# Selective-scan kernel: another table of places for the marks, the output additions, the convolution and the softplus

## The chip, the cores and the metric

One core of a Trainium2 chip runs the whole program. The metric is the time of one execution on the device in microseconds; smaller is better. The time of a run is that of this one core.

## The reference, cut to what matters

The input is x of 4 x 1024 tokens by 256. It is normalised over its last axis, and two branches start from it: eight Mamba layers, and a mixture of eight experts with one expert per token. The result is x + s * silu(g), with s from the Mamba branch and g from the experts. Only the Mamba branch is touched here. One layer is:

```python
xz = einsum('bld,ed->ble', x, Wi); xin, z = split(xz, 2)
xin = silu(causal_conv(xin, cw, cb))               # 4 taps, 512 channels
x_dbl = einsum('blc,ec->ble', xin, Wx)             # rank 16, B 16, C 16
delta = softplus(einsum('blr,cr->blc', dt_raw, Wdt) + bdt)
h = h * exp(d_t[..., None] * A) + (d_t * u_t)[..., None] * B_t[:, None, :]
y = einsum('bcn,bn->bc', h, C_t)                   # 16 states
y = (y + u * Dp) * silu(z)
x = x + einsum('blc,dc->bld', y, Wo)
```

## The kernel before, in words

The program has three blocks: `experts`, `mamba` and `finish`. `mamba` takes most of the time, and it alone changes.

**Units and steps.** `mamba` works in 64 units: 8 layers, 4 sequences, 2 halves of 512 tokens. Units with an even number start a sequence (h = 0), odd ones continue it (h = 1) and begin each scan from a carry. A unit has 64 steps, written (n, j): state n from 0 to 15, block j of 128 channels from 0 to 3. Step (n, j) is number k = 4n + j. While unit U is scanned, the same steps also prepare unit U+1 (the "late" work) and unit U+2 (the "early" work), and finish unit U-1. Every engine has one queue of instructions in order, and the order is written out by hand: at each step an engine does its regular work and then whatever the tables at the top of the file (L75 to L85) place there. A place with n of 16 or more belongs to the following unit, so (17, 0) is step (1, 0) of the next one.

**The regular work of a step.**
- GpSimd (POOL, L768) multiplies du by a broadcast row of B into one of 8 drive buffers, so it is at most 8 steps ahead of the scan.
- ScalarE (ACT, L800, `exponent`) writes the decay exp(delta * A) into one of two PSUM buffers `ps_d`. At step k it makes the decay of step k + 2 and waits for scan k.
- VectorE (DVE, L962, `scan`) does the scan of 512 tokens into `state`, which has two buffers of four blocks. The first scan of state n therefore waits until TensorE has turned all four tiles of state n - 2.
- TensorE (PE) turns a tile of the state of n - 1 into the ring `ps_r` (L1118, `turn_state`), and turns the weighted product back into `ps_y` (L1125, `turn_back`).
- ScalarE (L807, `weigh`) reads the ring, multiplies by C and writes `prod`.

**The ring.** `ps_r` has two PSUM buffers, used in turn by all that TensorE hands to ScalarE or VectorE. An item waits until the item two before it has been read. Between the turned states stand the other items, placed by `RING_AT` (L75): `X0` to `X3` and `Z0` to `Z3` (input projection), `C3` (the convolution of channel block 3, on TensorE), `XD` (L1185) and `BC` (the projection to rank, B and C), `DT0` to `DT3` (delta), `O0` and `O1` (output projection, L1206), `CNT` (a count of marks). ScalarE reads an item one step after its place; `CNT`, `O0` and `O1` are read by VectorE where `ALIVE_AT` and `ADD_AT` say.

**The other work on VectorE.** `mark_over` (L971, L973, `MARK_AT`) marks values over a limit; `CNT` sums the marks; `keep_alive` (L984, `ALIVE_AT`) turns the count into a mask; `add_x` (L1066, `ADD_AT`) adds an output block to the residual; `gate` (L1060, `GATE_AT`) makes the four gated blocks, for which `skip_y` on TensorE (`SKIPY_AT`) waits; `conv` (L997 for the first tap, L1001 for the other three, `CONV_AT`) does 12 instructions for channel blocks 0 to 2; `softplus` (L1020, L1023, L1027, L1030, `SOFT_AT`) has two times four parts; `make_du` (L1010, `DU_AT`) has two parts, and POOL's first drive of the next unit waits for the first part, its third drive for the second.

**The other work on ScalarE.** At `SILU_AT` it does silu of the convolution (`silu_u`, L835), silu of z (`silu_z`, L839) and loads the other table again (L913). `silu_u` waits for the last convolution instruction. In the queue, `exponent` of a step stands ahead of the silus and `weigh` behind them:

```python
exponent(U, h, k)                       # k = CB * n + t + 2
if (n, t) == SILU_AT:
    silu_u(U, kind, U + 1); silu_z(U, h, kind)
    nc.scalar.preload_act_table_set(TABLE)
late(...); early(...)
weigh(U, h, kind, ("S", n - 1, t), U, n - 1, t)
```

**The other work on POOL.** `halo` (L747, L749, `HALO_AT`) waits for the last convolution instruction and for `C3`; `mask_x` (L739, `XM_AT`) waits for `keep_alive`; `keep_carry` (L754) copies the last column of a state. All stand in one queue with the drives.

**SP's queue** issues the DMAs. In the first unit of a layer its load of w_out (L630) waits until `O1` is in the ring, and the rows of B for states 8 to 15 (`load_brep`, L654) stand behind it.

## Time and profile before

| what | value |
| --- | --- |
| median of 3 runs | 7821.57 us (7820.64 to 7832.61) |
| the profiled execution, its own time | 7820.31 us |
| its span, first to last instruction | 7818.5 us |
| granted TensorE clock, mean of the span | 0.991 |
| busy: PE, PEld, DVE, ACT, POOL | 6939.0, 4775.6, 6646.4, 6434.1, 5911.4 us |

The page of the profile gives each engine's busy time and share of the span. Four engines are busy between 76% and 89%, so no share alone names the bound. The views that do are the busy time by stretch (one unit at a time), the waits, and the order of instructions by time on each engine inside one unit. A row of the order by time has the start, the time from the first start to the last end, the engine, the line, what is written and read, and in brackets the idle time before it with what ended it.

### The profile page before, as it was taken

What the parts mean: (1) busy time and instruction counts of PE and PEld (TensorE: products, weight loads), DVE (VectorE), ACT (ScalarE), POOL (GpSimd) and SP (SyncE); (2) the same over time, 40 slices, a digit from 0 to 9 for tenths busy, and PEclk for the clock granted to TensorE, in tenths of its full rate; (3) what the DMA queues carried; (4) which work ended last, traced back from release to release, by engine and by line L of the source; (5) the groups of instructions that cost most, each with busy time, mean ns of one, the idle gap of its engine ahead of it and who ended that gap; (6) DMA issues with size and microseconds to landing.
All of it is one profiled execution on the core that took longest, in us unless ns stands there. A gap on an engine that the chain in (4) does not pass through costs nothing. (4 is left out here: it accounts for less than half of the span.)

```text
span 7818.5 us, 143762 instructions
## 1 busy us (share of the span) xinstructions
PE 6939.0 (89%) x40051; PEld 4775.6 (61%) x40051; DVE 6646.4 (85%) x6454; ACT 6434.1 (82%) x10306; POOL 5911.4 (76%) x4899
## 2 busy tenths in 40 slices
PE   4978999999989998999998998989999999999987
PEld 3646666666666666666666666666666666666665
DVE  2249888988988998889889888988898898889888
ACT  1238888888888888888888888888888888888886
POOL 2128878887878888788877887887888788887875
PEclk9989999999999999999999999999999999999998
DMA  5111111111111111111111111111111111111112
GB/s 172 34 39 39 39 38 47 44 39 39 42 44 42 39 39 42 47 40 40 39 47 42 38 40 41 46 42 38 40 47 42 39 38 42 44 43 38 41 37 89
DMA packets 226304, 355.78 MB, mean 46 GB/s; under 512 B 43680, under 2 KB 82368, under 8 KB 225376
## 3 DMA queue, kind: packets, MB, share of 16 engines
q1 hardware_dynamic: 222096, 336.91, 15.9%
q0 software_dynamic: 3408, 9.33, 0.3%
q8 instruction: 365, 5.98, 0.3%
q14 instruction: 435, 3.56, 0.2%
HBM read 325.00 MB, written 21.14 MB: 44 GB/s over the span
## 5 line engine op out<-in xcount | busy, mean ns | idle before, releaser
L768 POOL TENSOR_TENSOR drive<-du,brep 128x512 f32<-128x512 f32 x4096 | 5499.6, 1372 | 725.9 <-DVE du L1010 359.7
L800 ACT ACTIVATE ps_d<-delta,cur 128x512 f32<-128x512 f32 x4096 | 2845.3, 695 | 453.7 <-DVE state L962 434.8
L807 ACT ACTIVATE prod<-ps_r,bcT 128x512 f32<-128x512 f32 x4096 | 2807.7, 686 | 242.3 <-PE ps_r L1118 237.3
L1118 PE MATMUL ps_r<-ident,state 128*128 128x128 f32 x16384 | 2551.6, 279 | 321.8 <-ACT prod L807 176.1
L962 DVE TENSOR_TENSOR_SCAN state<-ps_d,carry,drive 128x512 f32<-128x512 f32 x2048 | 2503.0, 1264 | 310.6 <-PE ps_r L1118 275.9
L962 DVE TENSOR_TENSOR_SCAN state<-ps_d,drive 128x512 f32<-128x512 f32 x2048 | 2389.7, 1206 | 301.0 <-PE ps_r L1118 237.7
L1125 PE MATMUL ps_y<-ident,prod 128*128 128x128 f32 x16384 | 2467.5, 275 | 25.9 <-ACT prod L807 25.9
L1125 PEld LDWEIGHTS ps_y<-ident,prod 128*128 128x128 f32 x16384 | 1929.0, 142 | 664.7 <-issue 514.0
L1118 PEld LDWEIGHTS ps_r<-ident,state 128*128 128x128 f32 x16384 | 1834.4, 141 | 768.0 <-ACT prod L807 495.1
L1166 PE MATMUL ps_r<-xm,w_inz_sb 128*128 128x512 f32 x1024 | 508.9, 620 | 91.8 <-ACT prod L807 91.8
L1158 PE MATMUL ps_r<-xm,w_inx_sb 128*128 128x512 f32 x1024 | 508.3, 620 | 25.9 <-ACT prod L807 14.3
L1206 PE MATMUL ps_r<-relu,w_out_sb 128*128 128x512 f32 x1024 | 472.5, 604 | 59.9 <-ACT prod L807 57.2
L1001 DVE SCALAR_TENSOR_TENSOR xc<-xpad,taps,xc 128x512 f32<-128x512 f32 x576 | 513.9, 892 | 2.7
L754 POOL COPY carry<-state 128x4 f32<-128x4 f32 x512 | 222.5, 435 | 218.1 <-DVE state L962 215.9
L1199 PE MATMUL ps_r<-xdbl,w_dt_sb 16*128 16x512 f32 x512 | 291.0, 649 | 86.0 <-DVE xres L1066 41.7
L1206 PEld LDWEIGHTS ps_r<-relu,w_out_sb 128*128 128x128 f32 x1024 | 184.1, 189 | 273.4 <-issue 216.6
L1166 PEld LDWEIGHTS ps_r<-xm,w_inz_sb 128*128 128x128 f32 x1024 | 174.4, 190 | 272.3 <-ACT prod L807 136.9
L1158 PEld LDWEIGHTS ps_r<-xm,w_inx_sb 128*128 128x128 f32 x1024 | 175.3, 190 | 196.2 <-issue 153.8
L427 ACT ACTIVATE hid<-ps_t,b_sb 128x128 f32<-128x128 f32 x312 | 84.8, 382 | 225.5 <-PE ps_t L388 225.5
L1185 PE MATMUL ps_r<-u,w_x_sb 128*48 128x512 f32 x512 | 235.2, 603 | 34.2 <-ACT u L835 34.2
L355 POOL DMA_INDIRECT ys_dram<-yb,row x39 | 37.4, 959 | 292.6 <-DVE yb L447 292.6
L1136 PE MATMUL ps_y<-u,skip 128*128 128x512 f32 x512 | 241.6, 594 | 9.4 <-DVE relu L1060 9.3
(136 smaller groups left out, 4574.7 us busy)
## 6 DMA issues: line engine op xcount, KB each, us to landing
brep<-bc_dram SPq DMA_DIRECT2D x1024, 256.0 KB, 3.3
w_sb<-w SPq DMA_DIRECT2D x8, 1024.0 KB, 17.5
w_all<-w SPq DMA_DIRECT2D x8, 1024.0 KB, 12.7
xs_dram<-nothing SPq DMA_DIRECT2D x1, 5011.5 KB, 35.9
xb<-xs_dram SPq DMA_DIRECT2D x39, 128.5 KB, 2.0
w_all<-x SPq DMA_DIRECT2D x1, 4096.0 KB, 14.7
w_inx_sb<-w_in SPq DMA_DIRECT2D x8, 512.0 KB, 4.0
w_inz_sb<-w_in SPq DMA_DIRECT2D x8, 512.0 KB, 4.4
```

Source lines behind the costliest of these rows:

```text
L768: nc.gpsimd.tensor_tensor(drive[:, k % DRIVE, :], du[:, j, :], brep[:, n % BREP, :], ALU.mult).then_inc(drive_set, 1)
L800: nc.scalar.activation(ps_d[:, k % 2, :], delta[h][:, j, :], ACT.Exp, scale=cur[h][:, a:a + 1]).then_inc(decay_set, 1)
L807: nc.scalar.activation(prod[:, t, :], ps_r[:, item_place(U, h, kind, item), :], ACT.Copy, scale=bcT[(h + 1) % 2 if item[1] == "prev" else ...
L962: nc.vector.tensor_tensor_scan(state[n % 2][:, j, :], ps_d[:, k % 2, :], drive[:, k % DRIVE, :], carry[:, n, j:j + 1] if h == 1 else 0.0, ...
L1001: step = nc.vector.scalar_tensor_tensor(xc[:, j, :], xpad[:, j, tap:tap + T], w, xc[:, j, :], ALU.mult, ALU.add)
L1118: last = nc.tensor.transpose(out[:, j * P:(j + 1) * P], state[n % 2][:, j, t * P:(t + 1) * P], ident[:])
L1125: last = nc.tensor.matmul(ps_y[:, j, t * P:(t + 1) * P], prod[:, t, j * P:(j + 1) * P], ident[:], start=False, stop=True, is_transpose=Tru ...
L1136: last = nc.tensor.matmul(ps_y[:, j, :], skip[:, j, :], u[:, j, :], start=True, stop=True, skip_group_check=True)
L1158: last = nc.tensor.matmul(out, w_inx_sb[:, k, j * P:(j + 1) * P], xm[h][:, k, :], start=(k == 0), stop=(k == DB - 1))
L1166: last = nc.tensor.matmul(out, w_inz_sb[:, k, j * P:(j + 1) * P], xm[hf][:, k, :], start=(k == 0), stop=(k == DB - 1))
L1199: nc.tensor.matmul(out, w_dt_sb[:, j * P:(j + 1) * P], xdbl[0:RANK, :], start=True, stop=True).then_inc(ring_ready, 1)
L1206: last = nc.tensor.matmul(out, w_out_sb[:, j, k * P:(k + 1) * P], gated[:, j, :], start=(j == 0), stop=(j == CB - 1))
```

## The change

Only the tables of places change. No instruction is added or taken away and no shape changes; `LOW_AT` is a new name that nothing in the kernel reads. `SILU_AT` goes one step later. The marks, the alive mask and both additions come to lie at (3, 3) to (4, 3); the gates are all at (1, 1). The convolution of a unit begins at (6, 2) instead of (5, 2), and four of its 12 instructions instead of three lie in the next unit. `C3` goes from (1, 0) to (2, 3). The softplus begins at (9, 2) instead of (7, 3), and the second part of `make_du` goes from (14, 3) to (15, 2).

```diff
-RING_AT = {"CNT": (3, 0), "O0": (4, 1), "O1": (5, 3), "XD": (4, 2), "BC": (7, 3), "DT0": (6, 0), "DT1": (6, 2), "DT2": (8, 0),
-           "DT3": (9, 2), "Z0": (10, 1), "Z1": (11, 3), "Z2": (14, 1), "Z3": (15, 0), "X0": (5, 0), "X1": (8, 3),
-           "X2": (10, 3), "X3": (14, 2), "C3": (17, 0)}
-SILU_AT, EXP_AT, LN_AT = (4, 2), [(7, 0), (10, 1)], [(8, 3), (11, 3)]
-MARK_AT, ALIVE_AT, ADD_AT = [(2, 1), (2, 2)], (3, 1), [(4, 3), (6, 1)]
+RING_AT = {"CNT": (4, 0), "O0": (3, 3), "O1": (4, 2), "XD": (4, 3), "BC": (11, 3), "DT0": (7, 2), "DT1": (7, 3),
+           "DT2": (10, 2), "DT3": (10, 3), "Z0": (9, 1), "Z1": (9, 3), "Z2": (13, 3), "Z3": (15, 0), "X0": (5, 3),
+           "X1": (7, 0), "X2": (8, 3), "X3": (13, 0), "C3": (18, 3)}
+SILU_AT, EXP_AT, LN_AT = (4, 3), [(9, 0), (12, 1)], [(9, 1), (13, 0)]
+MARK_AT, ALIVE_AT, ADD_AT = [(3, 3), (4, 0)], (4, 2), [(4, 1), (4, 3)]
 PE_CONV, DVE_CONV = [3], [0, 1, 2]
-GATE_AT, SKIPY_AT = [(1, 1), (1, 2), (1, 2), (1, 2)], [(1, 1), (1, 3), (1, 3), (1, 3)]
-SOFT_AT = [(7, 3), (8, 3), (9, 3), (10, 2), (10, 3), (11, 3), (14, 2), (14, 3)]
-CONV_AT = [(5, 2), (5, 2), (6, 0), (6, 2), (9, 2), (10, 1), (12, 2), (12, 3), (15, 1), (17, 0), (17, 3), (19, 0)]
-DU_AT = [(14, 3), (14, 3)]
-HALO_AT, XM_AT = (3, 2), (5, 1)
+GATE_AT, SKIPY_AT = [(1, 1), (1, 1), (1, 1), (1, 1)], [(1, 2), (1, 2), (1, 3), (1, 3)]
+LOW_AT = [(4, 1), (8, 2)]
+SOFT_AT = [(9, 2), (9, 3), (10, 3), (12, 3), (13, 1), (13, 3), (14, 2), (14, 3)]
+CONV_AT = [(6, 2), (7, 2), (7, 3), (8, 0), (9, 0), (9, 2), (10, 2), (11, 1), (18, 2), (18, 2), (19, 2), (19, 3)]
+DU_AT = [(14, 3), (15, 2)]
+HALO_AT, XM_AT = (4, 2), (5, 2)
```

## Rows read from the trace of the kernel before

**Rows 1.** The page's busy time of each engine.

```profile
PE 6939.0 (89%) x40051; PEld 4775.6 (61%) x40051; DVE 6646.4 (85%) x6454; ACT 6434.1 (82%) x10306; POOL 5911.4 (76%) x4899
```

**Rows 2.** Units 26, 27: us; PE, PEld, DVE, ACT, POOL busy; clock, DMA, GB/s.

```profile
3477.70:3589.40 111.70, 101.78 (x600) 70.03 (x601) 99.53 (x97) 98.69 (x157) 90.53 (x82) 1.00 0.16 40
3589.40:3702.80 113.40, 101.97 (x601) 69.83 (x600) 102.12 (x95) 98.50 (x156) 91.16 (x68) 1.00 0.15 39
```

**Rows 3.** Waits over the whole span: total us, times, longest us.

```profile
DVE state L962 <- PE ps_r L1118: 513.6, 262, 11.1
...
DVE xres L1066 <- PE ps_r L1206: 138.8, 67, 3.9
```

**Rows 4.** Order by time on ScalarE in unit 26: at C3, around the silus.

```profile
3488.70 0.69 ACT L827 ACTIVATE xc<-ps_r,taps 128x512 f32<-128x512 f32 x1 [2.24 <-PE ps_r L1177]
...
3507.15 0.70 ACT L800 ACTIVATE ps_d<-delta,cur 128x512 f32<-128x512 f32 x1
3507.86 1.28 ACT L835 ACT_TABLE_LOAD   x1
...
3514.18 0.69 ACT L807 ACTIVATE prod<-ps_r,bcT 128x512 f32<-128x512 f32 x1
3514.77 0.69 ACT L800 ACTIVATE ps_d<-delta,cur 128x512 f32<-128x512 f32 x1
```

**Rows 5.** Order by time on VectorE: unit 23 at the silus, unit 26 to (7, 0).

```profile
3169.82 0.69 DVE L1066 TENSOR_TENSOR xres<-xres,ps_r 128x512 f32 x1 [1.80 <-PE ps_r L1206]
3175.66 3.63 DVE L962 TENSOR_TENSOR_SCAN state<-ps_d,carry,drive 128x512 f32<-128x512 f32 x3 [5.16 <-PE ps_r L1118]
...
3501.17 6.77 DVE L962 TENSOR_TENSOR_SCAN state<-ps_d,drive 128x512 f32<-128x512 f32 x6
3510.28 0.69 DVE L1066 TENSOR_TENSOR xres<-xres,ps_r 128x512 f32 x1 [2.34 <-PE ps_r L1206]
3515.98 3.45 DVE L962 TENSOR_TENSOR_SCAN state<-ps_d,drive 128x512 f32<-128x512 f32 x3 [5.01 <-PE ps_r L1118]
...
3531.84 3.45 DVE L962 TENSOR_TENSOR_SCAN state<-ps_d,drive 128x512 f32<-128x512 f32 x3 [1.90 <-PE ps_r L1118]
```

**Rows 6.** Order by time on TensorE in unit 26: C3, CNT, O0, XD, DT0.

```profile
3484.90 3.60 PE L1177 MATMUL ps_r<-xpad,conv_w 128*128 128x512 f32 x8
...
3498.86 1.04 PE L1149 MATMUL ps_r<-over_mark,minus_ones 128*128 128x512 bf16 x4
...
3506.38 3.67 PE L1206 MATMUL ps_r<-relu,w_out_sb 128*128 128x512 f32 x8 [0.77 <-ACT prod L807]
...
3511.22 3.61 PE L1185 MATMUL ps_r<-u,w_x_sb 128*48 128x512 f32 x8 [0.30 <-ACT u L835]
...
3526.42 1.12 PE L1199 MATMUL ps_r<-xdbl,w_dt_sb 16*128 16x512 f32 x2 [0.18 <-DVE xres L1066]
```

**Rows 7.** Durations in ns, min/median/max, of four of VectorE's lines.

```profile
L997 DVE TENSOR_SCALAR xc<-xpad,taps x192: 514/646/1928, 482.2 to 7550.3; 128x512 f32<-128x512 f32 x192
...
L1001 DVE SCALAR_TENSOR_TENSOR xc<-xpad,taps,xc x576: 716/752/5805, 482.7 to 7574.0; 128x512 f32<-128x512 f32 x192
...
L971 DVE TENSOR_SCALAR over_mark<-xres x64: 658/661/687, 470.2 to 7455.2; 128x1024 bf16 x60, 128x1024 bf16<-128x1024 f32 x4
...
L1020 DVE TENSOR_SCALAR low<-soft x128: 659/666/1661, 505.8 to 7633.5; 128x1024 f32<-128x1024 f32 x128
```

**Rows 8.** Order by time on VectorE: step (1, 0) of units 26 and 15.

```profile
3483.43 1.09 DVE L1001 SCALAR_TENSOR_TENSOR xc<-xpad,taps,xc 128x512 f32<-128x512 f32 x1
...
2235.38 5.80 DVE L1001 SCALAR_TENSOR_TENSOR xc<-xpad,taps,xc 128x512 f32<-128x512 f32 x1
```

**Rows 9.** Order by time on POOL: halo and mask in unit 26; drives in unit 24.

```profile
3499.06 0.11 POOL L749 MEMSET xpad<- 128x12 f32 x1 [6.86 <-DVE xc L1001]
...
3507.98 2.35 POOL L739 TENSOR_TENSOR xm<-xres,alive 128x1024 f32<-128x1024 f32 x1
...
3304.93 2.51 POOL L768 TENSOR_TENSOR drive<-du,brep 128x512 f32<-128x512 f32 x2 [6.10 <-DMA brep<-bc_dram]
```

## The prediction

> **What bounds the kernel now.** The page comes first: four engines between 76% and 89% [rows 1], so no share decides. Then one unit at a time: unit 26 takes 111.7 us with VectorE busy 99.5, the odd unit 27 takes 113.4 with VectorE busy 102.1 [rows 2]. Period less busy is what VectorE stands idle: 12.2 and 11.3 us. ScalarE and TensorE stand 13 and 10 us idle, so the engines take turns at being late. The clock is 1.00 in both. Where VectorE has scans alone they follow each other at 1.11 us (six in 6.77, [rows 5]); ScalarE's pair for the same step, weigh and decay, takes about 0.6 us each (0.59 from one to the next, [rows 4]), nearly the same. So each unit is a chain over three queues, and its length is VectorE's busy time plus VectorE's waits. The waits view says for what: 513.6 us for turned states, 138.8 for output blocks [rows 3].
>
> The largest wait has one place. ScalarE leaves its pairs at 3507.15 + 0.71, loads a table, does both silus, loads the table back and is at the next weigh at 3514.18: 7.03 us from the start of the last decay to the next weigh [rows 4]. Meanwhile VectorE waits 2.34 us for O0 and 5.01 us for the last turned tile of state 3, 7.35 us; in an odd unit 1.80 + 5.16 [rows 5]. Mean 7.15. The rest of the idle time, 4 to 5 us, lies behind: 1.90 us behind O1 and DT0 [rows 5], and small ones of 0.7 us and less.
>
> **The change part by part.** No instruction comes or goes, and VectorE's work stays some 100 us; a part gains only by shortening a wait of VectorE's or its contention.
>
> *The silus one step later.* VectorE can get past ScalarE's absence only as far as decays and turned tiles allow. Before, the silus follow the decay of (5, 0), and the last tile of state 3 waits in the ring for a weigh behind the silus, so scan (5, 0) waits too: one scan and O0's addition lie in the gap. After, the silus follow the decay of (5, 1) and the weigh of (4, 2) is done ahead of them, so the tile comes out while ScalarE is away: O1's addition (0.6) and the scans (5, 0) and (5, 1) lie in the gap. From the end of scan (4, 3) to scan (5, 2): 7.03 + 0.59 (weigh) + 0.69 (decay) + 0.1 = 8.4 us; VectorE has 0.6 + 2 x 1.13 = 2.8 for it; 5.6 us idle, and 0.2 more as ScalarE comes late to the decay. O1 (3.67 on TensorE, [rows 6]) is ready 3.2 us into this, before it costs more. 5.8 against 7.15: **-1.35 us a unit**. The marks, the mask and the first addition stand ahead of scan (4, 3), on which the silus' decay waits: they are next to the silus, not beside them, and gain nothing there.
>
> *The stretch ahead of the silus.* Before it costs VectorE 0.1 us in waits. Now C3 is at (2, 3), O0 at (3, 3), CNT at (4, 0), O1 at (4, 2). C3 used to lie beside the gates and two convolution instructions. From the end of scan (2, 2): decay 0.75 with ScalarE's lateness of 0.15, weigh 0.7, C3 3.65 [rows 6], its read and the next weigh 1.15, decay 0.7, and some 0.2 of handing over, 7.3 us to scan (3, 3). VectorE has for it two convolution instructions (0.5 + 0.8), four scans (4.5) and one more convolution (0.7), 6.5: it waits 0.8 to 0.9. O0 starts when the weigh of (3, 2) is done; its 3.7 us end 0.25 us after VectorE reaches the addition. CNT's buffer is the one O0 leaves, so the count starts only behind that addition and takes 1.2 + 0.2 [rows 6]; VectorE has one scan for it and waits 0.4. Sum 1.5 in an even unit, 1.2 in an odd one (scans 0.06 longer give TensorE time): **+1.25**.
>
> *From (5, 2) to the end.* The wait behind O1 and its addition (1.90) goes; in its place come X0 at (5, 3) (waits of 0.6 and 0.8 around it) and DT0 and DT1 side by side at (7, 2) and (7, 3), right behind X1: DT0 1.05, its read 1.3, one buffer for both, a wait of 1.3. With the small ones at X2, Z0, DT2, DT3 and the later EXP and LN I come to 5.1 in an even unit and some 4.3 in an odd one, against 4.6: **+0.1**.
>
> *Contention.* A convolution instruction (L1001) takes 0.72 us at least, 1.09 beside drives at (1, 0) [rows 7, 8]. (1, 0) and (1, 3) lie beside unbroken drives; (3, 2) and (3, 3) now come near POOL's wait at the halo. But the marks, 0.66 each and now all in POOL's idle 6.86 us [rows 7, 9], lose that cover. Bounds -1.5 and +2.5; I take **-0.5**, near the 0.3 + 0.3 of the two moved instructions.
>
> *POOL and SP.* The halo goes behind drive 18 and waits for (3, 3): POOL is then 3 steps ahead of the scan and does four drives (1.25 each, two in 2.51, [rows 9]) while VectorE does three scans and 3 us of other work; the mask waits for the alive mask 2 us more, but ScalarE's absence gives POOL 5 us to catch up. The second du at (15, 2) stops the third drive until then: it ends about 2 us before its scan. Both cost nothing; without that slack each us late is a us of the unit. In the first unit of a layer SP's load of w_out waits for O1, and POOL waits 6.10 us for a row of B [rows 9]; O1 comes some 12 us sooner, so that goes. It cost VectorE 0.5 to 1 us, seven times: **-4 in all**.
>
> *The long ones.* In units 15, 33, 37 and 61 the instruction at (1, 0) takes 5.80 us [rows 8], 20 us in all. Nothing of its kind stands there any more. It may come elsewhere; I take -15, bounds -20 and +20.
>
> Sum a unit: -1.35 + 1.25 + 0.1 - 0.5 = -0.5, over 62 units -31; with -4 and -15, -50. Against the profiled execution's own 7820.3 us (span 7818.5, 1.8 around it) that is 7770; the median of the runs is 1.3 higher, which changes nothing. About 0.2%, 16 us, is what a measurement here tells from no change.
>
> **A rule that speaks against it.** The size shows in L997, also one VectorE operation with a scalar per partition: it takes 0.51 to 1.93 us, while the mark, beside an idle POOL, never exceeds 0.69 [rows 7]. The Trainium skill (SBUF — State Buffer, "SBUF: two separate sides") has it that VectorE and GpSimd share one pair of ports under a lock held for a whole instruction, the other blocking fully; by that, marks moved from POOL's idle time beside its drives can each wait out a drive. This stands below as a rival.
>
> **The rivals.**
> - *Forecast*: waits change places, small gain, 7735 to 7805. Chance 0.38.
> - *The waits of the front stretch are covered.* If ScalarE and TensorE come out of the gates (2.4 us of VectorE's work that needs neither) ahead by more than I reckon, C3 and O0 cost 0.2 instead of 1.25, and DT0 waits less: -1.35 + 0.2 - 0.4 - 0.6 = -2.2 a unit, -136, and -24 in all for SP and the long ones: 7660. For it: ScalarE waits 2.24 us at C3 before, and VectorE does not notice [rows 4]. Chance 0.22.
> - *Slower by the convoy on TensorE.* O0, CNT and O1 are 3.5 + 1.2 + 3.5 us in four steps whose scans take 4.5, each holding a ring buffer that VectorE frees. If O0 starts later than scan (4, 0), each us goes straight through addition, count, mask and scan (4, 3) to the silus. At 1.5 us later: +1.0 a unit in sum, +62 - 19: 7863. Against it: convolution, marks and scans at (3, 2) to (4, 0) give it time. Chance 0.17.
> - *The lock.* One mark waits out a drive, 1.93 - 0.51 = 1.4 us more: +0.9 a unit, 7857; both marks, +2.3, 7944. For it: the halo releases POOL just at the marks. Against it: L1020, as large and mostly beside drives, has a median of 0.67 [rows 7]. Chance 0.09.
> - *No change*: what the gap gains the front takes, contention as before: -0.0 a unit, 7820. That the change does less than its words say belongs here: only one of five moved items lies in the gap. Chance 0.14.
>
> **How the numbers follow.** Faster: 0.33 of the forecast, the covered case, 0.02 of the last: 0.57. Same: 0.05 and 0.10, 0.15. Slower: 0.17 + 0.09 + 0.02, 0.28. The range, 7670 to 7875, leaves out half of the covered case and both marks in the lock; the likeliest case's own is 7735 to 7805.
>
> **What would show it.** Right: one addition and then two scans between table load and table load on VectorE, with waits of 3 and 2 us around them instead of 2.3 and 5.0; waits of 0.9 before scan (3, 3), below 0.5 before the first addition and the alive scan; about 1.3 at (8, 0); no wait of POOL for brep; no scan that waits for a drive; even periods near 111, odd near 113. Wrong: the wait at the silus over 6.5 us; the first addition waiting over 1 us; marks of 1.5 us and more; scans that wait for drives; or a granted clock that falls, since 1.00 holds in both units [rows 2].

## The result, and the profile after

The changed kernel takes **8008.3 us** (median of four runs, 8000.6 to 8013.4) against 7821.1 (7816.9 to 7832.6) for the kernel before in the same runs: a ratio of 1.0236, 95% interval 1.0222 to 1.0251. It is slower, and the time lies outside the range of the forecast.

The page's busy time of each engine in the kernel after:

```profile
PE 7005.9 (87%) x39987; PEld 4911.3 (61%) x40051; DVE 6856.5 (86%) x6454; ACT 6424.7 (80%) x10306; POOL 5868.9 (73%) x4899
```

The profiled span grew from 7818.5 to 8009.8 us, by 191. VectorE's busy time grew by 210 with the same 6454 instructions [rows 1], so it stands idle 19 us less than before. The waits did not make the kernel slower; VectorE's instructions became longer. Which ones, the groups by line say (busy us, mean ns, then the idle time before them; every line number is one higher than before):

```profile
L1002 DVE SCALAR_TENSOR_TENSOR xc<-xpad,taps,xc 128x512 f32<-128x512 f32 x576 | 526.3, 914 | 2.8
L998 DVE TENSOR_SCALAR xc<-xpad,taps 128x512 f32<-128x512 f32 x192 | 329.3, 1715 | 15.8 <-ACT xpad L814 14.0
L1031 DVE TENSOR_TENSOR delta<-low,relu 128x1024 f32<-128x1024 f32 x128 | 166.6, 1301 | 0.1
L1024 DVE TENSOR_TENSOR low<-soft,low 128x1024 f32<-128x1024 f32 x128 | 158.8, 1241 | 0.1
L1021 DVE TENSOR_SCALAR low<-soft 128x1024 f32<-128x1024 f32 x128 | 103.5, 809 | 17.3 <-ACT soft L870 17.3
```

and the same groups before:

```profile
L1001 DVE SCALAR_TENSOR_TENSOR xc<-xpad,taps,xc 128x512 f32<-128x512 f32 x576 | 513.9, 892 | 2.7
L1023 DVE TENSOR_TENSOR low<-soft,low 128x1024 f32<-128x1024 f32 x128 | 178.6, 1396 | 0.1
L997 DVE TENSOR_SCALAR xc<-xpad,taps 128x512 f32<-128x512 f32 x192 | 169.5, 883 | 32.1 <-ACT xpad L813 32.0
L1030 DVE TENSOR_TENSOR delta<-low,relu 128x1024 f32<-128x1024 f32 x128 | 153.1, 1196 | 0.1
L1020 DVE TENSOR_SCALAR low<-soft 128x1024 f32<-128x1024 f32 x128 | 89.4, 699 | 15.2 <-ACT soft L869 15.1
```

One group stands out: the first tap of a convolution step (L998) gains 160 of the 210 us, though its median is 0.63 us as before. Its longest are the answer (min/median/max in ns):

```profile
L998 DVE TENSOR_SCALAR xc<-xpad,taps x192: 521/626/5196, 479.5 to 7759.8; 128x512 f32<-128x512 f32 x192
```

They all stand at step (2, 2), where the change puts the third first tap of a unit. There it takes over 4 us in 28 of 32 even units (median 4.43) and 5.16 us in 21 of 31 odd ones. Unit 27, in order of time on VectorE:

```profile
3688.57 1.26 DVE L963 TENSOR_TENSOR_SCAN state<-ps_d,carry,drive 128x512 f32<-128x512 f32 x1
3689.75 5.20 DVE L998 TENSOR_SCALAR xc<-xpad,taps 128x512 f32<-128x512 f32 x1
3694.98 0.75 DVE L1002 SCALAR_TENSOR_TENSOR xc<-xpad,taps,xc 128x512 f32<-128x512 f32 x1
3695.65 4.80 DVE L963 TENSOR_TENSOR_SCAN state<-ps_d,carry,drive 128x512 f32<-128x512 f32 x4
...
3702.85 0.69 DVE L972 TENSOR_SCALAR over_mark<-xres 128x1024 bf16 x1
...
3704.64 0.71 DVE L974 TENSOR_SCALAR over_mark<-xres 128x1024 bf16 x1
...
3707.01 0.69 DVE L1067 TENSOR_TENSOR xres<-xres,ps_r 128x512 f32 x1 [0.46 <-PE ps_r L1207]
...
3709.22 1.28 DVE L985 TENSOR_TENSOR_SCAN alive<-ps_r,alive,zeros 128x512 f32<-128x512 f32 x1 [0.33 <-PE ps_r L1150]
...
3714.80 0.69 DVE L1067 TENSOR_TENSOR xres<-xres,ps_r 128x512 f32 x1 [3.12 <-PE ps_r L1207]
3715.57 2.46 DVE L963 TENSOR_TENSOR_SCAN state<-ps_d,carry,drive 128x512 f32<-128x512 f32 x2
3720.19 1.28 DVE L963 TENSOR_TENSOR_SCAN state<-ps_d,carry,drive 128x512 f32<-128x512 f32 x1 [2.16 <-ACT ps_d L801]
```

and the same stretch on POOL, of unit 27 and of unit 28 (there the tap runs from 3807.00 to 3811.44):

```profile
3673.54 4.97 POOL L769 TENSOR_TENSOR drive<-du,brep 128x512 f32<-128x512 f32 x4 [1.85 <-DVE du L1011]
...
3678.59 16.07 POOL L769 TENSOR_TENSOR drive<-du,brep 128x512 f32<-128x512 f32 x13
3703.27 0.32 POOL L748 COPY xpad<-xpad 128x12 f32<-128x12 f32 x1 [8.61 <-PE ps_r L1119]
...
3806.17 4.97 POOL L769 TENSOR_TENSOR drive<-du,brep 128x512 f32<-128x512 f32 x4
3813.52 0.19 POOL L755 COPY carry<-state 128x4 f32<-128x4 f32 x1 [2.38 <-DVE state L963]
```

POOL makes its drives back to back until something makes it wait: in unit 27 the row ends at 3678.59 + 16.07 = 3694.66, in unit 28 at 3811.14. The tap ends at 3694.95 and at 3811.44, **0.3 us after the end of the row** both times. It starts beside a drive, three to four drives before the row ends, and does not come in at any of the boundaries between. The other ten odd units have the same row, and there the tap comes in at the first boundary, after 1.47 to 1.50 us: a long tap is frequent at this place, not certain. Where POOL's row is short or POOL has just waited, the same instruction takes 0.5 to 0.9 us.

The rest of the unit stands nearly as forecast: marks of 0.69 and 0.71, one addition and two scans between the table loads, with waits of 3.12 and 2.16 around them in place of 1.80 and 5.16 [rows 5]. TensorE pays a little too: it waits for what the tap holds up, and runs its next matmuls at half speed.

```profile
3691.26 3.70 PE L1178 MATMUL ps_r<-xpad,conv_w 128*128 128x512 f32 x8 [0.53 <-ACT prod L808]
...
3698.31 1.12 PE L1119 MATMUL ps_r<-ident,state 128*128 128x128 f32 x4 [2.91 <-ACT prod L808]
```

The matmul behind the 2.91 us takes 1.12 where the same ones before it take 0.60. Over the stretch from the tap on (us; PE, PEld, DVE, ACT, POOL busy; clock, DMA share, GB/s) the granted clock is 0.86, so part of it ran at 1.2 instead of 2.4 GHz:

```profile
3689.70:3702.20 12.50, 9.06 (x43) 6.49 (x42) 12.46 (x9) 6.29 (x11) 4.96 (x5) 0.86 0.05 21
```

The mean granted clock of the span is 0.967 (0.991 before), and 0.97 and 0.99 in units 27 and 28. It is 0.970 in an experiment below that is 100 us faster, so those 100 us are not the clock's. Whether it has a part in the rest no run shows.

### The profile page after: what moved, and what is told of

The parts are those of the page before. It is cut to its first block and busy times, and to the rows that moved or that the text cites. A ratio compares the mean times of both kernels' runs of the same rounds, so it can differ in the third digit from the quotient of the medians.

```text
span 8009.8 us, 143698 instructions
## 1 busy us (share of the span) xinstructions
PE 7005.9 (87%) x39987; PEld 4911.3 (61%) x40051; DVE 6856.5 (86%) x6454; ACT 6424.7 (80%) x10306; POOL 5868.9 (73%) x4899
## 5 line engine op out<-in xcount | busy, mean ns | idle before, releaser
L1119 PE MATMUL ps_r<-ident,state 128*128 128x128 f32 x16384 | 2608.4, 284 | 357.0 <-ACT prod L808 256.2
L1126 PE MATMUL ps_y<-ident,prod 128*128 128x128 f32 x16384 | 2541.7, 280 | 25.8 <-ACT prod L808 25.8
L1126 PEld LDWEIGHTS ps_y<-ident,prod 128*128 128x128 f32 x16384 | 1996.7, 145 | 703.5 <-issue 485.5
L1119 PEld LDWEIGHTS ps_r<-ident,state 128*128 128x128 f32 x16384 | 1907.1, 145 | 701.9 <-ACT prod L808 491.6
L998 DVE TENSOR_SCALAR xc<-xpad,taps 128x512 f32<-128x512 f32 x192 | 329.3, 1715 | 15.8 <-ACT xpad L814 14.0
L1067 DVE TENSOR_TENSOR xres<-xres,ps_r 128x512 f32 (+1 forms) x128 | 87.5, 684 | 230.5 <-PE ps_r L1207 230.5
L1178 PE MATMUL ps_r<-xpad,conv_w 128*128 128x512 f32 x512 | 236.0, 603 | 40.6 <-ACT prod L808 39.8
```

Source lines behind the costliest of these rows:

```text
L998: step = nc.vector.tensor_scalar(xc[:, j, :], xpad[:, j, tap:tap + T], w, taps[h][:, COL_CB + j:COL_CB + j + 1], ALU.mult, ALU.add)
L1119: last = nc.tensor.transpose(out[:, j * P:(j + 1) * P], state[n % 2][:, j, t * P:(t + 1) * P], ident[:])
L1126: last = nc.tensor.matmul(ps_y[:, j, t * P:(t + 1) * P], prod[:, t, j * P:(j + 1) * P], ident[:], start=False, stop=True, is_transpose=Tru ...
```

## The experiments

The theory after the result: **a VectorE instruction whose operands lie in SBUF is shut out by POOL's drives, and at (2, 2) to the end of the row.** Rivals: that it is the kind of instruction, C3's reads of xpad on TensorE beside it, or the convolution's move being harmless and something else in the change costing the time.

**Another instruction first at (2, 2).** The first tap goes back to (15, 1), a later tap now stands first at (2, 2).

```
-CONV_AT = [..., (18, 2), (18, 2), (19, 2), (19, 3)]
+CONV_AT = [..., (15, 1), (18, 2), (19, 2), (19, 3)]
```

> The changed kernel with the first tap of the last channel block moved back from (2, 2) to (15, 1) of the unit before, where it stood in the kernel before; the second tap stays at (2, 2). Theory A (the first tap, a tensor_scalar in SBUF, cannot start inside POOL's unbroken row of drives): it takes 0.5 to 0.6 us at (15, 1), the instruction left at (2, 2), a scalar_tensor_tensor, gets in between two drives in about 1 us, and the unit loses 4 us: VectorE busy about 6590 us, time 7770 to 7800. Theory B (it is the place beside C3, which reads the same tile on TensorE, that is slow): the second tap now takes 4 to 5 us at (2, 2), time about 8000. Theory C (the long instruction only fills time that C3 and the ring need anyway): VectorE waits for a decay or a turned tile instead, time above 7900.

8012.6 us, ratio to the kernel before 1.0225 (1.0195 to 1.0255): not the 7770 to 7800 of theory A. The long instruction stays, it is only another one now (unit 28, VectorE and POOL):

```profile
3804.76 4.69 DVE L1002 SCALAR_TENSOR_TENSOR xc<-xpad,taps,xc 128x512 f32<-128x512 f32 x1
...
3803.94 4.96 POOL L769 TENSOR_TENSOR drive<-du,brep 128x512 f32<-128x512 f32 x4
```

It ends at 3809.45, 0.55 us after POOL's 3808.90. The kind of instruction does not decide; the place does. Theory A was wrong in that the second kind would get in, and this run leaves theory B standing. A first tap alone ends 0.28 behind POOL, a later tap 0.55.

**An earlier halo, so a shorter row.**

```
-HALO_AT, XM_AT = (4, 2), (5, 2)
+HALO_AT, XM_AT = (4, 0), (5, 2)
```

> The changed kernel with the halo at (4, 0) instead of (4, 2), so POOL's row of drives ends two drives sooner in odd units (after drive 16, not 18) and one sooner in even ones, where a carry copy that waits ends it after drive 17. Theory A (the first tap starts when the row ends): 5.16 us become about 2.6 in odd units, 4.43 become about 3.2 in even ones; time 7870 to 7910. Theory B (C3 beside it): both unchanged, time about 8005.

7939.9 us (one run). POOL's row ends earlier and the tap with it: median 3.21 in even and 2.71 in odd units. The length follows the row's end, as the theory has it. The time missed the expected 7870 to 7910, and a new place has its share in that: the first tap at (6, 2) takes 2.49 to 2.58 us in all 31 odd units, where it takes 0.6 in the changed kernel. POOL has by then run 20.9 us without a pause; the tap misses one boundary and ends 0.28 us behind the end of the row.

**C3 back at (17, 0), away from the taps.**

```
-           ..., "X3": (13, 0), "C3": (18, 3)}
+           ..., "X3": (13, 0), "C3": (17, 0)}
```

> The changed kernel with C3 back at (1, 0). Theory A (POOL's drives): the first tap at (2, 2) keeps its 4.4 and 5.2 us, time 7990 to 8020. Theory B (C3's reads of the same tile hold the first tap): it falls to 0.5 to 1 us, time about 7750.

7988.9 us (one run). C3 now costs waits of 3.05 and 2.66 us ahead of (2, 0), so the tap begins later and lasts 1.2 to 1.35 (even) and 2.41 us (odd), yet it still ends 0.28 behind the row. The expected 4.4 and 5.2 us did not come, since the row's end is nearer when the tap begins. With C3 elsewhere the tap still misses a boundary in 31 of 31 odd units, so TensorE's reads of xpad are not what shuts it out.

**The kernel before with the new places of the taps.**

```
-CONV_AT = [..., (15, 1), (17, 0), (17, 3), (19, 0)]
+CONV_AT = [..., (18, 2), (18, 2), (18, 3), (19, 0)]
```

> The kernel before with its last four convolution instructions at (2, 2), (2, 2), (2, 3) and (3, 0) instead of (15, 1), (1, 0), (1, 3) and (3, 0). POOL stands idle at the halo there, from about (1, 3) on. Theory A (only unbroken drives hold the first tap up): it takes 0.5 to 0.6 us at (2, 2), the four long instructions at (1, 0) are gone, time 7790 to 7830. Theory that the step or the unit's phase makes it slow, whatever POOL does: 4 to 5 us at (2, 2), time about 8080.

7902.9 us, ratio 1.0083 (1.0054 to 1.0112); the expectation missed. No tap is long at (2, 2): with the old halo at (3, 2) POOL already stands still there. The 5.80 us at (1, 0) are gone as well. What it costs is cover: the taps at (1, 0) and (1, 3) used to lie beside C3, and without them VectorE waits 1.41 and 1.09 us ahead of (2, 0).

**The change with the old places of the taps.**

```
-CONV_AT = [..., (18, 2), (18, 2), (19, 2), (19, 3)]
+CONV_AT = [..., (15, 1), (17, 0), (17, 3), (19, 0)]
```

> The change with its four last convolution steps at the places that they had before, all else changed. Theory (the 190 us come from the first tap at (2,2) that now meets GpSimd's unbroken row): no first tap over 1.6 us at (2,2), since none stands there; in its place the O and C3 waits ahead of (2,3) to (5,1) have no taps as cover, 1.5 to 2.5 us a unit beyond the change's 5.5, and the long instruction's 2.9 to 3.9 us a unit are gone: 7880 to 7950, between the two kernels. Rival (the move of marks, alive mask and additions is what costs, not the convolution): the time stays at 7990 to 8010.

8012.2 us, ratio 1.0256 (1.0221 to 1.0291): no gain at all, and my range missed. No tap exceeds 1.86 us:

```profile
L998 DVE TENSOR_SCALAR xc<-xpad,taps x192: 521/637/1482, 484.2 to 7738.9; 128x512 f32<-128x512 f32 x192
...
L1002 DVE SCALAR_TENSOR_TENSOR xc<-xpad,taps,xc x576: 718/856/1851, 484.8 to 7763.4; 128x512 f32<-128x512 f32 x192
```

But a wait of 1.9 to 2.0 us for C3 appears ahead of (3, 3), and taps at (1, 0), (9, 2) and (11, 1) are lengthened by single drives. So is the first mark, at (3, 3): 1.16 us in even and 1.20 in odd units, all of them, against 0.66 before. That is the lock rival of the prediction, for one mark and at a third of its price. VectorE is busy 6744.5 us, 98 more than before, and idle 94 more. So the long tap is not a sum on top of the rest: where it stands, it hides C3's wait, and where the taps are elsewhere that wait and other lengthened taps cost as much. The tap had to be cured where it stands.

**POOL yields.** In the changed kernel POOL waits ahead of drive 15 until VectorE has done the two taps at (2, 2). It has the time, being three to four drives ahead there.

```
+                        if k == 15 and kind != "last":
+                            pool.wait_ge(conv_step, 9 * F + 8)
```

> The changed kernel, where POOL waits before its drive 15, that of step (3, 3), until both convolution instructions of (2, 2) are done. POOL has 4 to 9 us to spare there, since it waits at the halo afterwards anyway. Theory A (the first tap can start only when POOL lets go, and POOL's row of drives need not let go): it takes 0.5 to 0.8 us in every unit; the waits of the prediction come to light, C3's 0.9 us before scan (3, 3) among them; unit pairs fall from 232.3 to about 226 us; time 7800 to 7840, within half a per cent of the kernel before. Rival (the long instruction is only the visible part of a longer wait for C3 and the ring): the waits before (3, 3) take 3 us or more and the time stays above 7900.

7908.3 us, ratio to before 1.0117 (1.0059 to 1.0175), so 100 us less than the changed kernel. Unit 27 on VectorE and POOL:

```profile
3652.43 0.52 DVE L1000 TENSOR_SCALAR xc<-xpad,taps 128x512 f32<-128x512 f32 x1
3652.99 0.75 DVE L1004 SCALAR_TENSOR_TENSOR xc<-xpad,taps,xc 128x512 f32<-128x512 f32 x1
...
3658.38 0.94 DVE L1004 SCALAR_TENSOR_TENSOR xc<-xpad,taps,xc 128x512 f32<-128x512 f32 x1
3659.87 1.28 DVE L965 TENSOR_TENSOR_SCAN state<-ps_d,carry,drive 128x512 f32<-128x512 f32 x1 [0.55 <-ACT ps_d L803]
...
3641.28 11.14 POOL L771 TENSOR_TENSOR drive<-du,brep 128x512 f32<-128x512 f32 x9
3653.82 4.95 POOL L771 TENSOR_TENSOR drive<-du,brep 128x512 f32<-128x512 f32 x4 [1.41 <-DVE xc L1004]
```

A pause of 1.41 us on POOL turns the 5.20 us into 0.52 (0.74 in even units). VectorE's busy time falls to 6668.0, 188 less than in the changed kernel, while the span falls by 103: the other half comes back as waits that the long tap had covered (0.55 to 0.66 ahead of (3, 3), 0.8 and 1.1 ahead of (8, 3) and (9, 0) in even units). My 7800 to 7840 counted the first of them and not the others.

**A second yield** ahead of drive 45, for the tap at (9, 2), which takes 1.76 us in odd units.

```
+                        if k == 45 and kind in ("first", "mid"):
+                            pool.wait_ge(conv_step, 9 * G + 5)
```

> As the run before, and POOL also waits before drive 45 until the second tap of block 1 at (9, 2) is done, which takes 1.76 us in the changed kernel beside a drive that has just begun. Theory A: it takes 0.72 to 0.8 us, 1.0 us a unit less on VectorE; time 7740 to 7800. If ScalarE and TensorE bound that stretch, the wait comes back at (9, 3) or (10, 0) and the time is that of the run before.

7901.9 us (two runs), not the 7740 to 7800 of the theory but nearly the time of the run before: that tap is short, but the one at (10, 2) now takes 1.41 to 1.63, and a wait of 0.4 appears ahead of (10, 0). The saving comes back next door.

**The same idea in the kernel before**, for the taps at (1, 0) and at (5, 2) (1.90 us there in odd units).

```
+                        if k == 9 and kind != "last":
+                            pool.wait_ge(conv_step, 9 * F + 8)
+                        if k == 29 and kind in ("first", "mid"):
+                            pool.wait_ge(conv_step, 9 * G + 2)
```

> The kernel before, where POOL waits before drive 9 for the convolution instruction of (1, 0) and before drive 29 for the two of (5, 2). Theory A: no instruction at (1, 0) takes 5.8 us, four times 4.9 us gone; the first tap at (5, 2) falls from 1.90 to 0.5 us in odd units and from 0.77 to 0.5 in even ones. If VectorE bounds the stretch behind (5, 2), 7750 to 7775; if the wait before (7, 0), which follows from O1 on TensorE, takes it back, 7795 to 7805.

**7759.1 us** (ten runs, 7754.5 to 7764.6), ratio 0.992 (0.9901 to 0.994): faster than both kernels, with no step of the order changed. The 5.80 us at (1, 0) no longer occur:

```profile
L1005 DVE SCALAR_TENSOR_TENSOR xc<-xpad,taps,xc x576: 716/829/1642, 482.4 to 7516.9; 128x512 f32<-128x512 f32 x192
...
L1001 DVE TENSOR_SCALAR xc<-xpad,taps x192: 509/546/1594, 481.8 to 7492.7; 128x512 f32<-128x512 f32 x192
```

The longest was 5.805 us, the first tap's median 646 ns [rows 7]. The four long ones are the smaller part of the gain: they gave VectorE back 20 us, the first tap at (5, 2) in odd units, 1.90 us before and 0.55 now, gave it 40.

**Why is the first boundary missed?** Small kernels try it alone; nothing of the reference is computed in them. POOL makes rows of drives that never wait, VectorE follows with scans and then, beside the row, one tap. The first has 22 rows and no ScalarE.

> Only the disputed thing: 22 trials, in each a row of 16 drives on POOL that never waits, and on VectorE 2 to 12 scans, then one first tap (trials 1 to 11) or one later tap (trials 12 to 22), then the other scans; nothing on ScalarE and TensorE, nothing of the reference is computed and the output is the input. Theory A1 (a lock that POOL gives up at the end of each drive): every tap ends 0.3 to 0.6 us after the drive in which it came, 0.6 to 1.8 us long. Theory A2 (POOL keeps the port as long as its next drive is ready): taps last until the row ends, up to 17 us for the early ones, in all trials or in those that start at certain points of a drive. Rival: 0.5 and 0.7 us throughout, and the long ones need ScalarE or TensorE beside them. Time about 600 us.

Every first tap takes 1.55 us and every later tap 1.81: they wait out one drive and come in. Up to 15.9 us, the longest that POOL had run here before a tap, an unbroken row shut nothing out. The second adds waits on POOL and ScalarE's exponentials.

> Nothing of the reference is computed; the output is the input. 24 rows of 20 drives on GpSimd, never held up; VectorE starts six drives later, makes 8 scans, a copy from PSUM to PSUM of 8 to 480 columns that shifts the phase, and then one first tap (SBUF operands) while GpSimd is in the middle of its row. The groups: GpSimd without and with a wait (always satisfied) ahead of each drive, ScalarE idle or making the exponentials beside it. Theory A (VectorE gets in at the end of the drive that is under way, whatever the phase): every first tap takes 0.3 us more than what is left of the current drive, 0.3 to 1.6 us, in all four groups. Rival B (a tap that comes late in a drive misses the first boundary and is kept out to the end of the row): the taps of some phases take over 5 us, those of others under 1.6. Rival C (the waits between drives, or ScalarE's instructions, are what shuts VectorE out): long taps in the groups that have them and none in the first group. I expect C at 0.4, A at 0.35, B at 0.25.

Without ScalarE none of twelve is long; with it three of twelve, 8.25, 7.86 and 5.82 us, with POOL's waits or without. ScalarE's phase was swept next, coarsely and then finely.

> Nothing of the reference is computed. In the kernel before this one the first tap was shut out to the end of GpSimd's row in 3 of 12 trials with ScalarE's exponentials beside it and in 0 of 12 without; in all twelve with them an exponential ended 0.01 to 0.02 us after the boundary between two drives. Here 80 rows of 16 drives; VectorE (and with it ScalarE) starts later by 33 ns more each time, so that the end of the exponential passes over the whole of a drive; in the first 40 rows the exponential reads SBUF, in the last 40 PSUM. Theory (the first boundary is missed where ScalarE's access to SBUF ends or begins right at it): some of the first 40 taps over 3 us, all at a few neighbouring offsets of the exponential's end or start to the boundary, and none of the last 40. Rival A (any instruction of ScalarE at the boundary does it, through its signal): the same offsets in both halves. Rival B (chance, whatever the offset): long taps scattered over all offsets in the first half. I give the theory 0.5, A 0.2, B 0.15, and 0.15 that none is shut out.

> Nothing of the reference is computed. In the sweep before this one no tap was shut out, but its offsets jumped over the very place: the exponential's end stood at 0.21 us before the boundary between two drives and further off, or at 0.06 us after it and more, while the three taps shut out in the kernel with 24 rows all had it 0.01 us after. Here 135 rows: 45 starts of VectorE in steps of 8 ns, which bring the exponential's end from 0.21 us before to 0.15 us after the boundary, twice with ScalarE reading SBUF and once reading PSUM alone. Theory (the boundary is missed when ScalarE's access to SBUF ends within some 30 ns of it): of the first 90 taps 2 to 15 over 3 us, all with the end of the exponential between 0.02 before and 0.04 after the boundary, at the same offsets in both passes, and none of the last 45. Rival A (ScalarE's signal or any instruction of it): the last 45 have them too. Rival B (chance, not tied to ScalarE's end): long taps scattered over the offsets, or none. Theory 0.45, A 0.25, B 0.3.

None of 80 (longest 1.70 us) and none of 135 (1.15): no offset of ScalarE does it. These rows were shorter, with the tap after four scans, so the old arrangement was repeated.

> Nothing of the reference is computed. 75 rows of 20 drives, VectorE six drives behind, 8 scans and a short copy ahead of the first tap, as in the kernel of 24 rows that had three taps shut out; 30 rows with the copy stepped by 16 columns, 15 with VectorE starting later by 33 ns steps, 30 with ScalarE reading PSUM alone. Theory (ScalarE's reading of SBUF is needed, and with it the miss comes at a rate of about a quarter, by nothing that the trace shows): 5 to 15 of the first 45 over 3 us, 0 of the last 30. Rival A (any instruction of ScalarE will do): the last 30 have 4 to 12. Rival B (it goes with an offset of a few ns): the long ones of the first 30, whose exponential stands at one offset, are all or none, and those of the next 15 lie side by side. Rival C: the three were rare chances, at most 2 of 75. Theory 0.4, A 0.2, B 0.15, C 0.25.

20 of 45 are long with the exponential on SBUF and 0 of 30 with it on PSUM, which looked like an answer. The next crossed it with the offset and the arrangement.

> Nothing of the reference is computed. The kernel before this one had 20 long taps of 45 with ScalarE's exponential reading SBUF and 0 of 30 with it reading PSUM, but the latter all ended 0.1 us earlier against the boundary, at one offset; and the two sweeps without a long tap differed in three things (row of 16, VectorE five drives behind, tap after 4 scans). 108 rows of 20 drives: 30 starts of VectorE in steps of 33 ns with ScalarE reading PSUM; the same 30 with it reading SBUF; and 16 each with SBUF and (five behind, 4 scans), (five behind, 8 scans), (six behind, 4 scans). Theory (reading SBUF is needed): 0 of the first 30, 8 to 20 of the next 30. Rival A (an offset that the PSUM rows had not met): long ones in the first 30 too. For the last three groups: if the length of the row was the difference, all three have long taps; if the number of scans, only the middle one; if VectorE's distance behind POOL, only the last. Theory 0.7; row 0.25, scans 0.35, distance 0.25.

13 of 30 with PSUM, 19 of 30 with SBUF: the answer was wrong. After four scans none of 32; after eight and five drives behind, 2 of 16. So it goes with how far the row has come.

> Nothing of the reference is computed. The kernel before this one had 13 of 30 taps shut out with ScalarE on PSUM and 19 of 30 with it on SBUF after 8 scans, none of 32 after 4 scans. 78 rows of 20 drives, VectorE six drives behind: 30 offsets with ScalarE idle and the tap after 8 scans, then 16 offsets each with ScalarE's exponentials and the tap after 6, 8 and 10 scans. Theory (some other engine's instructions are needed, of any kind, and the miss becomes likelier the longer the row has run): 0 of the first 30; then about 1, 6 and 10 of 16. Rival A (ScalarE not needed, its absence before was chance): 8 or more of the first 30. Rival B (the number of scans acts through one place in the program, such as the tile that is being read, not through the length of the row): 8 scans alone have long taps, 6 and 10 none. Theory 0.5, A 0.1, B 0.25, 0.15 other.

With ScalarE idle 11 of 30 are long, so it is not needed at all; after 6, 8 and 10 scans it is 0, 13 and 16 of 16. The last small kernel parts POOL's row from VectorE's scans.

> Nothing of the reference is computed. So far, with rows of 20 drives: taps that start while drive 12 or an earlier one is under way were shut out in 2 of some 160 trials, those beside drives 13 and 14 in about half, those beside drive 15 in 16 of 16; ScalarE is not needed (11 of 30 with it idle). 64 rows of 24 drives, 16 offsets each: tap after 4 scans with VectorE twelve drives behind (beside drive 16 or so); after 8 scans, two behind (beside drive 10); after 10 scans, six behind (beside drive 15); and the last once more with GpSimd waiting 0.7 to 1.2 us ahead of drive 10 for the sixth scan. Theory (what counts is how long GpSimd has run unbroken): 14 to 16 long in the first group, none in the second, 16 in the third, none in the fourth, where the tap comes some 5 drives after the pause. Rival (what counts is VectorE's own number of scans since its last use of SBUF alone): none, 8, 16, 16. A rival inside the theory (a pause doesn't start the count anew): 16 in the fourth. Theory 0.6 (with the pause counting, 0.45), rival 0.25.

16 of 16 long after four scans beside drives 15 and 16, 0 of 16 after eight beside drive 9, 16 of 16 after ten beside drive 15, and **0 of 16 for the same with a pause**. VectorE, a row of the third and one of the fourth group, then POOL beside them:

```profile
1368.58 10.80 DVE L105 TENSOR_SCALAR xc<-xpad,w 128x512 f32<-128x512 f32 x1
...
2202.55 0.87 DVE L105 TENSOR_SCALAR xc<-xpad,w 128x512 f32<-128x512 f32 x1
```

```profile
1349.76 29.34 POOL L52 TENSOR_TENSOR drive<-du,brep 128x512 f32<-128x512 f32 x24 [2.27 <-DVE w L112]
...
2183.62 12.25 POOL L52 TENSOR_TENSOR drive<-du,brep 128x512 f32<-128x512 f32 x10 [4.93 <-DVE w L112]
2196.98 17.33 POOL L52 TENSOR_TENSOR drive<-du,brep 128x512 f32<-128x512 f32 x14 [1.10 <-DVE state L92]
```

The first tap comes 18.8 us after its row began and ends at 1379.38, 0.28 us behind the row's end; the second comes as late in its trial, but 5.6 us after a pause of 1.10 us. What counts is how long POOL has run since it last paused or let VectorE in; every drive takes 1.23 us, so no run tells the time from the number of drives. Counted over the traces, for VectorE instructions with no PSUM operand that find at least two more drives to come, a pause being 0.3 us or more: in the small kernels 0 of 320 are shut out below 15.5 us, 81 of 218 from 15.5 to 18, 48 of 48 above 18.5; in the ten kernels of full size tried up to then 1 of some 5,600 below 8 us, 4 of 59 at 8 to 9 us, which are the 5.80 us of the kernel before, and 127 of 152 at 15 to 17. The two sets agree in the course and not at 8 us, and what sets the four apart no run shows. The full kernels add more where only one more drive is to come: above 18.5 us the tap misses the boundary in 120 of 122 cases. And a pause shorter than 0.3 us seems to do: the first tap at (6, 2) of odd units comes 16.0 us after POOL's last longer pause but 3.5 us after one of 0.26 to 0.30, and none of 210 such taps, over seven kernels, is shut out. In unit 27 of the changed kernel POOL runs on from 3673.54 and VectorE reads or writes PSUM in all that it does until the tap at 3689.75: 16.2 us.

**The test of it in the full kernel**: one tap moved so that it breaks the 16 us, POOL's row left alone.

```
-CONV_AT = [..., (18, 2), (18, 2), (19, 2), (19, 3)]
+CONV_AT = [..., (17, 0), (18, 2), (19, 2), (19, 3)]
```

> The changed kernel with one tap instruction moved: the first tap from (2, 2) to (1, 0), the next one stays at (2, 2). Taken over all runs so far, an instruction of VectorE on SBUF alone was shut out for more than one drive in 1 of some 5,600 cases when GpSimd had run less than 8 us since it last paused or let such an instruction in, in 4 of 59 at 8.x us, and in 127 of 152 at 15 to 17 us; in the changed kernel 16 us pass before (2, 2). Theory (this time is what counts): with the tap at (1, 0) VectorE gets in after some 9 us and again at (2, 2) after some 6; at most 5 long ones at (1, 0), none at (2, 2); C3's wait shows again (0.5 ahead of (3, 3)), and the time falls to 7890 to 7950 like that with GpSimd's pause. Rival (the place (2, 2) or the length of GpSimd's row decides, whatever came in between): the tap left at (2, 2) takes 4.7 and 5.4 us as it did with the first tap at (15, 1), and the time stays at 8000 to 8020.

7910.5 us, ratio 1.0094 (1.0077 to 1.0111): about 98 us less than the changed kernel by one instruction's place. Unit 27 on VectorE and on POOL:

```profile
3628.62 1.09 DVE L998 TENSOR_SCALAR xc<-xpad,taps 128x512 f32<-128x512 f32 x1
...
3639.09 0.93 DVE L1002 SCALAR_TENSOR_TENSOR xc<-xpad,taps,xc 128x512 f32<-128x512 f32 x1
...
3626.92 16.68 POOL L769 TENSOR_TENSOR drive<-du,brep 128x512 f32<-128x512 f32 x13
```

The row is as long as in the changed kernel, and the tap at (2, 2) takes 0.93 us in odd and 1.55 in even units where it took 5.4 and 4.7 in the first experiment. One of 63 is still long (4.01 us), after 9.0 us. The gap, 9.0 to 10.7 us, was longer than the 6 us that I expected, since the tap at (1, 0) comes in early. C3's wait ahead of (3, 3) is 1.15 us, not the expected 0.5.

## Why the prediction was wrong

The sum of the forecast was -50 us, the result is +190. The first three points compare VectorE's idle time in a stretch, even and odd unit, with that before.

- **The gap at the silus, -1.35.** Before 7.35 and 6.96; after 5.52 and 5.37, so -1.7. The mechanism was right, and the waits have the forecast sizes, 3.12 and 2.16 in unit 27 against "waits of 3 and 2 us"; the new gap was reckoned at 5.8 and is 5.45.
- **The stretch ahead of the silus, +1.25.** Measured +0.7. The first addition waits 0.47 and 0.21 (forecast 0.25), the alive scan 0.49 and 0.33 (0.4). C3's 0.8 to 0.9 did not show, because the long tap gave TensorE 4 us. With the tap cured it is 0.66 and 0.55; with the taps at their old places, one of them left ahead of it, 2.0. So C3's term was right in kind and a third too large.
- **From (5, 2) to the end, +0.1.** Measured +0.9 in even and odd units alike. DT0 waits 1.34 and 1.26 (forecast 1.3); the waits ahead of (11, 3) and (12, 0), 1.2 and 1.8 us together, were counted among "the small ones" and are the size that was missed. With the tap cured the even units have 2.6 more than before here.
- **The waits in all** come to -0.3 us a unit where the forecast had 0.0.
- **Contention, -0.5 with bounds -1.5 and +2.5: this is the step that failed.** VectorE's 210 us are +3.4 a unit, outside the step's own bounds. I priced a tap beside drives from 0.72 and 1.09 us and bounded it by one drive. The trace of before held the larger price, 5.80 us [rows 8], four times, and I booked it as an oddity of the place (1, 0): "Nothing of its kind stands there any more". Each of the four comes after 8.5 us of POOL unbroken with no SBUF-only instruction of VectorE, as do the 27 other odd units, which lose nothing. The same trace held the miss far more often, and I misread it: the 1.93 us of the first tap [rows 7] is not the price of one drive. It stands at (5, 2) of odd units. Unit 27 before, on VectorE and POOL:

```profile
3631.43 1.91 DVE L997 TENSOR_SCALAR xc<-xpad,taps 128x512 f32<-128x512 f32 x1 [0.20 <-ACT xpad L813]
...
3610.86 0.20 POOL L747 COPY xpad<-xpad 128x12 f32<-128x12 f32 x1 [6.95 <-DVE xc L1001]
3611.00 8.66 POOL L768 TENSOR_TENSOR drive<-du,brep 128x512 f32<-128x512 f32 x7
3619.61 2.36 POOL L739 TENSOR_TENSOR xm<-xres,alive 128x1024 f32<-128x1024 f32 x1
3621.93 11.13 POOL L768 TENSOR_TENSOR drive<-du,brep 128x512 f32<-128x512 f32 x9
```

POOL has run 20.6 us from its halo on. The tap misses the boundary at 3631.82 and ends at 3633.34, 0.28 us behind the row's end at 3633.06. It does so in 28 of 29 such units, and costs only 1.4 us because the row ends one drive later. The change takes the taps at (1, 0), (1, 3) and (3, 0) out of POOL's row and puts the halo's pause behind the rest, and so makes a stretch of 16 us ahead of (2, 2), with three to four more drives to come. That this stretch doubles could be read from the two orders. How often it costs that much could not, but a bound to the end of POOL's row, 4 to 5 us in each of 62 units, would have held the result.
- **The long ones, -15.** They are gone from (1, 0), worth 20 us as reckoned, and came back 49 times at (2, 2).
- **POOL and SP, -4.** POOL's seven waits of 5.5 to 6.1 us for brep are gone; too small to be told apart. The halo and the mask were harmless to POOL, as forecast, but not to VectorE: while POOL waits at the old halo, VectorE's taps are free of it.
- **The rivals.** The lock had the right cause and the wrong victim: in the changed kernel both marks stay at 0.69 to 0.71, the first beside a POOL that waits 8.61 us at the halo. With the taps at their old places the first mark did take 1.16 to 1.20. The Trainium skill (SBUF — State Buffer, "SBUF: two separate sides"), on which that rival rested, has the pair of ports held for one whole instruction; the runs agree in that no GpSimd instruction is cut, but VectorE waits out up to nine of them, not one. By one alone the tap at (2, 2) would take at most 1.5 us, as the undisturbed ones do, and it takes 4.4 to 5.2. The convoy on TensorE did not come; the covered front stretch did come in part, bought with the tap that covered it.
- **The signs.** Two that were named for being wrong came: the granted clock fell below 1.00 in both units, and five scans between units 1 and 61 wait 1.2 to 1.6 us for a drive.

How much of the 190 us is the tap? Freed of it, by POOL's pause or by the moved tap, the changed kernel gains 98 to 100 us by the medians, 93 and 111 by the ratios to the kernel before in the same runs; the remaining 80 to 90 show as waits and single-drive contention of the new order, and how much of them the lower clock makes is open. With the taps at their old places the change costs 198 without any long tap. So even with the right price for the tap, or with it cured, the change is slower than before, and no experiment shows its order of work to be worth its price.

## What to carry to other kernels

Where GpSimd works in SBUF without a pause, give VectorE an SBUF-only instruction at least every 8 us, or give GpSimd a short wait that it can afford (0.8% here, with four lines in the kernel before); past 15 us the next such instruction may wait to the end of GpSimd's row. Read an instruction's maximum before its median, and ask of each long one at which boundary it ended: 5.80 us in four units and 1.90 in 28 were the same thing, once with four drives left in the row and once with one. And what a stall covered becomes a wait when it goes: of the 3.0 us a unit that the pause took off VectorE's instructions, 1.4 came back as waits.

## What the runs showed of the hardware that was not expected

- Between VectorE on SBUF alone and GpSimd the boundary of an instruction is not always a chance to get in: after 15.5 to 18 us of GpSimd unbroken it is missed in 81 of 218 cases of the small kernels, after 18.5 us in 48 of 48 there and 120 of 122 in the full ones, and then every later one too, to the end of the row; up to 10.80 us for an instruction of 0.5.
- A pause starts the count anew (0 of 16 shut out after one of 1.0 to 1.5 us, 0 of 210 after one of 0.26 to 0.30), and so does an instruction of VectorE that got in (1 of 63 at (2, 2) against 49 of 63). Whether the count is of time or of drives, and why the first boundary is missed after it, no run shows.
- VectorE's instruction ends a fixed time after GpSimd's: 0.28 us for the first tap, 0.55 for a later one. Scans, with one operand in PSUM, keep their 1.2 to 1.27 us beside the same drives.
